# Expert tiles that add into shared rows: waits by token range, and an earlier copy out

## What is computed

```
logits = xf @ Wg.T
topw, topi = top_k(softmax(logits), 2)      # two experts per token
topw = topw / topw.sum(-1)
for e in range(16):
    h = silu(xf @ W1[e]) * (xf @ W3[e])
    out = out + gates[:, e:e+1] * (h @ W2[e])
x = x + out
```

## Time and profile before

| | |
|---|---|
| median of 3 runs | 940.09 us (938.54 to 945.49) |
| the profiled execution | 942.03 us, of which its span 940.3 us |
| mean granted TensorE clock | 0.938 of full |
| busy share PE / DVE / ACT / POOL | 87% / 65% / 42% / 43% |
| adding scatters on POOL (L647) | 80, 124.8 us in all |

### The profile page before, as it was taken

The page is one execution under the profiler, slowest core; times in us unless marked ns, Lnnn a source line. Parts: engine busy times, 40 slices in busy tenths (PEclk is TensorE's granted clock), DMA queues, the critical chain, the costliest instruction groups (busy, mean ns, idle before and its releaser), DMA issues.

```text
span 940.3 us, 19852 instructions
## 1 busy us (share of the span) xinstructions
PE 821.2 (87%) x5656; PEld 737.8 (78%) x5657; DVE 611.1 (65%) x1711; ACT 394.6 (42%) x1070; POOL 406.8 (43%) x583
## 2 busy tenths in 40 slices
PE   6899999999999999999999999986429998888840
PEld 6788999899989998999989999976317877766730
DVE  4446687877878777878787778766465554444520
ACT  5252553634526436245264462532334443333420
POOL 4212134344352533534434435235464456546661
PEclk9799999999999999999999999987559999999985
DMA  8960145172460642725517336086324665656657
GB/s 266 342 217 2 55 170 193 56 247 104 143 236 24 233 158 89 247 71 176 211 36 247 127 120 236 13 257 162 83 66 90 116 105 98 101 91 108 106 59 196
DMA packets 89602, 132.88 MB, mean 141 GB/s; under 512 B 6432, under 2 KB 54240, under 8 KB 89312
## 3 DMA queue, kind: packets, MB, share of 16 engines
q1 hardware_dynamic: 62944, 99.82, 31.9%
q0 software_dynamic: 14848, 19.41, 12.4%
q10 hardware_dynamic: 11776, 13.24, 5.1%
HBM read 37.42 MB, written 99.23 MB: 145 GB/s over the span
## 4 chain that ended last, share of the span: by engine, by line
PE 43%; ACT 15%; DVE 13%; issue 10%; DMA 8%; POOL 6%; ACTq 1%; SPq 1%; POOLq 0%; DVEq 0%
PE ps L656 37%; DMA row_sums<-narrow,sidx 7%; ACT phi L1066 5%; PE ps L663 4%; ACT fT_hi L1079 4%; ACT relu_v L1080 3%; POOL row_sums L647 3%; DVE nmax L1386 1%; DVE xrow_full L1421 1%; DVE smax L1428 1%; DVE row_max_of L1430 1%; DVE prT_lo L1281 1%; ACT pr L1122 1%; ACT qT_hi L1101 1%; DVE stat L1263 1%
## 5 line engine op out<-in xcount | busy, mean ns | idle before, releaser
L647 POOL DMA_INDIRECT row_sums<-narrow,sidx x80 | 124.8, 1560 | 97.9 <-DVE sidx L1611 55.7
L656 PE MATMUL ps<-e_sb,narrow 128*128 x320 | 113.0, 477 | 17.6 <-DVE narrow L1593 15.7
L656 PEld LDWEIGHTS ps<-e_sb,narrow 128*128 128x128 f32 x320 | 55.9, 195 | 38.5 <-issue 21.7
L1066 ACT ACTIVATE phi<-ps,nmax 128x128 f32<-128x128 f32 x256 | 71.3, 379 | 21.0 <-DVE nmax L1386 20.9
L656 PE MATMUL ps<-w_hi,fT_hi 128*128 128x256 f32 x256 | 78.2, 306 | 0.1
L656 PE MATMUL ps<-hT_hi,w_hi 128*128 128x256 f32 x256 | 73.3, 286 | 1.5 <-DVE hT_lo L1281 1.5
L1281 DVE TENSOR_TENSOR fT_lo<-relu_v,fT_hi 128x512 fp32r<-128x512 f32 x64 | 54.9, 858 | 27.4 <-ACT relu_v L1080 27.4
L656 PE MATMUL ps<-hT_hi,w_lo 128*128 128x256 f32 x256 | 72.5, 283 | 0.0
L656 PE MATMUL ps<-hT_lo,w_hi 128*128 128x256 f32 x256 | 72.5, 283 | 0.0
L656 PE MATMUL ps<-w_hi,fT_lo 128*128 128x256 f32 x256 | 72.2, 282 | 0.0
L656 PE MATMUL ps<-w_lo,fT_hi 128*128 128x256 f32 x256 | 72.1, 282 | 0.0
(11 more groups left out here) (269 smaller groups left out, 2699.0 us busy)
## 6 DMA issues: line engine op xcount, KB each, us to landing
expert_rows<-zero_rows SPq DMA_DIRECT2D x16, 4352.0 KB, 15.9
narrow<-expert_rows ACTq DMA_DIRECT2D x80, 136.0 KB
e_sb<-in_E SPq DMA_DIRECT2D x4, 1408.0 KB, 11.5
X<-in_x SPq DMA_DIRECT2D x16, 256.0 KB, 3.0
ctx_raw<-in_ctxT SPq DMA_DIRECT2D x16, 256.0 KB, 16.0
row_sums<-X SPq DMA_DIRECT2D x16, 256.0 KB, 2.2
raw_w<-in_W SPq DMA_DIRECT2D x2, 1024.0 KB, 6.8
e2a_lo<-in_E SPq DMA_DIRECT2D x1, 2048.0 KB
```

What stands on the lines that cost most here:

```text
L647: pool.indirect_dma_start(sum_dram, bass.IndirectOffsetOnAxis(sidx[:, u:u + 1], 0), yg[:, u, :], None, compute_op=ALU.add).then_inc(scatte ...
L656: return pe.matmul(out_, lhsT, rhs, start=start, stop=stop)
L1066: last = act.activation(phi[:, g, h, :], ps[:, g, h * M:(h + 1) * M], ACT.Exp, bias=nmax[:, g, h:h + 1])
```

## The change

1. `added_need` for s-1 and s-2 takes in whether the token ranges meet. For this, DVE computes the numbers of the first and the last row of each slot tile (`edge_i`), POOL gathers these rows from `expert_rows`, PE turns their target rows onto one partition (before tile 1), and DVE compares last row of s with first row of s-k (`meeting_tiles`, after tile 1); a tile that isn't full counts as reaching to the end. SP waits for it (`ranges_ready`) before tile 1.
2. In the last 8 tiles the unconditional wait for s-3 becomes one that holds only if tile s is real.
3. SP issues the first eight row loads in place of ACT.
4. SP waits, for each buffer, only for the real tiles (`landed_need`), and issues all 16 copies. ACT still waits for all scatters and all copies at the end.

```
@@ sync
             sp.wait_ge(x2_stored, 16 * NSEQ)
+            sp.wait_ge(zeroed, 16 * (NSEQ + 1))
             sp.wait_ge(plan_ready, 1)
+            sp.wait_ge(placed, NSEQ * 16 * TOPK * TS)
+            for s in range(GB):
+                tile = sp.value_load(tile_i[0:1, bass.ds(s, 1)], ...)
+                sp.dma_start(xg[:, s, :], row_tiles[...]).then_inc(rows_loaded[s], 16)
...
                 early = s if isinstance(s, int) and s < ADDING else ADDING
-                if early == ADDING:
+                if isinstance(s, int) and s == 1:
+                    sp.wait_ge(ranges_ready, 1)
+                if early == ADDING and not last:
                     v = (u - ADDING) % GB
                     hold(sp, scattered[v], rows_added(s - ADDING, v))
-                near = range(1, min(early, ADDING - 1) + 1)
+                near = range(1, (ADDING if last else min(early, ADDING - 1)) + 1)
...
             for u in range(GB):
-                sp.wait_ge(scattered[u], 16 * (SLOT_TILES // GB + 1))
-            for n in range(0, COPIES, 2):
+                need = sp.value_load(landed_need[0:1, u:u + 1], ...)
+                hold(sp, scattered[u], need)
+            for n in range(COPIES):
                 sp.dma_start(out_parts[n], sum_parts[n]).then_inc(out_stored, 16)
@@ gpsimd
             pool.memset(hid, 0.0).then_inc(hid_zero, 1)
+            pool.wait_ge(edges_ready, 1)
+            pool.wait_ge(placed, NSEQ * 16 * TOPK * TS)
+            for o in range(2):
+                pool.indirect_dma_start(edge[:, o, :], None, row_dram,
+                    bass.IndirectOffsetOnAxis(edge_i[:, o:o + 1], 0)).then_inc(edges_loaded, 16)
@@ tensor, slot_tiles
+                if isinstance(s, int) and s == 1:
+                    pe.wait_ge(edges_loaded, 16 * 2)
+                    for o in range(2):
+                        last_mm = mm(ps[0:1, 1, (2 + o) * P:(3 + o) * P], edge[:, o, D:D + 1], ident[:, :])
+                    last_mm.then_inc(edge_ps, 1)
+                if isinstance(s, int) and s == 3:
+                    pe.wait_ge(edges_read, 1)
@@ scalar
-            act.wait_ge(zeroed, 16 * (NSEQ + 1))
-            act.wait_ge(placed, NSEQ * 16 * TOPK * TS)
...
-            for s in range(GB):
-                load_rows(s, s)
...
-            for n in range(1, COPIES, 2):
-                act.dma_start(out_parts[n], sum_parts[n]).then_inc(out_stored, 16)
             act.wait_ge(out_stored, 16 * COPIES)
@@ vector
+            dve.wait_ge(row_ready, 1)
+            then(dve.tensor_scalar(row_c[:, :], row_g[:, :], float(ROW_TILES - 1), float(P), ALU.min, ALU.mult))
+            dve.tensor_copy(edge_i[:, 0:1], row_c[:, :])
+            dve.tensor_scalar(edge_i[:, 1:2], row_c[:, :], float(P - 1), None, ALU.add).then_inc(edges_ready, 1)
...
+            dve.tensor_scalar(real[:, :], ps[0:1, 1, 0:SLOT_TILES], float(NE), None, ALU.is_lt)
+            dve.tensor_scalar(expert_i[:, :], ..., ALU.min).then_inc(plan_ready, 1)
...
+            dve.scalar_tensor_tensor(added_need[:, ADDING - 1, ADDING:], real[:, ADDING:], 16.0,
+                                     round_of[:, 0:SLOT_TILES - ADDING], ALU.mult, ALU.add)
+            then(dve.tensor_tensor(real_late[:, :], real[:, SLOT_TILES - 2 * GB:SLOT_TILES - GB],
+                                   real[:, SLOT_TILES - GB:], ALU.add))
+            then(dve.tensor_scalar(landed_need[:, :], real_late[:, :], 16.0,
+                                   float(16 * (NT * TOPK // GB + 1)), ALU.mult, ALU.add))
+            def meeting_tiles():
+                dve.wait_ge(edge_ps, 1)
+                dve.tensor_copy(edge_row[:, :, :], ps[0:1, 1, 2 * P:4 * P]...).then_inc(edges_read, 1)
+                dve.wait_ge(edges_read, 1)
+                firsts, lasts = (edge_row[:, o, :] for o in range(2))
+                then(dve.tensor_scalar(no_last[:, :], lasts, 0.0, float(DUMP + NT * P), ALU.is_equal, ALU.mult))
+                then(dve.tensor_tensor(last_row[:, :], lasts, no_last[:, :], ALU.add))
+                for k in range(1, ADDING):
+                    last = dve.tensor_tensor(meeting[:, k - 1, k:], last_row[:, k:], firsts[:, 0:SLOT_TILES - k], ALU.is_ge)
+                then(last)
+                for k in range(1, ADDING):
+                    last = dve.tensor_tensor(meeting[:, k - 1, k:], meeting[:, k - 1, k:], other_expert[:, k - 1, k:], ALU.mult)
+                then(last)
+                for k in range(1, ADDING):
+                    last = dve.scalar_tensor_tensor(added_need[:, k - 1, k:], meeting[:, k - 1, k:], 16.0,
+                                                    round_of[:, 0:SLOT_TILES - k], ALU.mult, ALU.add)
+                last.then_inc(ranges_ready, 1)
```

More of the change, by code:

```diff
@@ L160, in decoder @@
         round_of = sb("round_of", [1, SLOT_TILES])
-        other_expert = sb("other_expert", [1, 2, SLOT_TILES])
+        other_expert = sb("other_expert", [1, ADDING - 1, SLOT_TILES])
+        real = sb("real", [1, SLOT_TILES])
+        real_late = sb("real_late", [1, GB])
+        landed_need = sb("landed_need", [1, GB], I32)
+        row_c = sb("row_c", [P, 1])
+        edge_i = sb("edge_i", [P, 2], I32)
         first_round = sb("first_round", [16, GB, GB])
-        added_need = sb("added_need", [1, 2, SLOT_TILES], I32)
+        added_need = sb("added_need", [1, ADDING, SLOT_TILES], I32)
         early_scope = ExitStack()
@@ L237, in decoder @@
         xg = carve(GB * RW).rearrange("p (u w) -> p u w", u=GB)
+        edge = carve(2 * RW).rearrange("p (o w) -> p o w", o=2)
+        edge_row = carve(2 * SLOT_TILES)[0:1].rearrange("p (o t) -> p o t", o=2)
+        meeting = carve((ADDING - 1) * SLOT_TILES)[0:1].rearrange("p (k t) -> p k t", k=ADDING - 1)
+        no_last, last_row = (carve(SLOT_TILES)[0:1] for _ in range(2))
         yg = carve(GB * D).rearrange("p (u d) -> p u d", u=GB)
@@ L300, in decoder @@
         sidx_ready = sem("sidx_ready")
+        edges_ready, edges_loaded, edge_ps, edges_read, ranges_ready = (sem(n) for n in (
+            "edges_ready", "edges_loaded", "edge_ps", "edges_read", "ranges_ready"))
         rows_loaded = [sem(f"rows_loaded{u}") for u in range(GB)]
@@ L437, in _, with need_of @@
             sp.wait_ge(x2_stored, 16 * NSEQ)
+            sp.wait_ge(zeroed, 16 * (NSEQ + 1))
             sp.wait_ge(plan_ready, 1)
+            sp.wait_ge(placed, NSEQ * 16 * TOPK * TS)
+            for s in range(GB):
+                tile = sp.value_load(tile_i[0:1, bass.ds(s, 1)], min_val=0, max_val=ROW_TILES - 1)
+                sp.dma_start(xg[:, s, :], row_tiles[:, bass.ds(tile, 1), :].rearrange("p t w -> p (t w)"))\
+                    .then_inc(rows_loaded[s], 16)
             def rows_added(s, u):
                 return (s - u) * PER + 16 * 2
+            def need_of(k, s):
+                return sp.value_load(added_need[0:1, k - 1, bass.ds(s, 1)], min_val=16,
+                                     max_val=16 * (SLOT_TILES // GB + 1))
             def slot_tiles(s, u, last):
                 early = s if isinstance(s, int) and s < ADDING else ADDING
-                if early == ADDING:
+                if isinstance(s, int) and s == 1:
+                    sp.wait_ge(ranges_ready, 1)
+                if early == ADDING and not last:
                     v = (u - ADDING) % GB
                     hold(sp, scattered[v], rows_added(s - ADDING, v))
-                near = range(1, min(early, ADDING - 1) + 1)
-                needs = [sp.value_load(added_need[0:1, k - 1, bass.ds(s, 1)], min_val=16,
-                                       max_val=16 * (SLOT_TILES // GB + 1)) for k in near]
+                near = range(1, (ADDING if last else min(early, ADDING - 1)) + 1)
+                needs = [need_of(k, s) for k in near]
                 for k, need in zip(near, needs):
@@ L459, in _ @@
             for u in range(GB):
-                sp.wait_ge(scattered[u], 16 * (SLOT_TILES // GB + 1))
-            for n in range(0, COPIES, 2):
+                need = sp.value_load(landed_need[0:1, u:u + 1], min_val=16 * (NT * TOPK // GB + 1),
+                                     max_val=16 * (SLOT_TILES // GB + 1))
+                hold(sp, scattered[u], need)
+            for n in range(COPIES):
                 sp.dma_start(out_parts[n], sum_parts[n]).then_inc(out_stored, 16)
@@ L641, in _ @@
             pool.memset(hid, 0.0).then_inc(hid_zero, 1)
+            pool.wait_ge(edges_ready, 1)
+            pool.wait_ge(placed, NSEQ * 16 * TOPK * TS)
+            for o in range(2):
+                pool.indirect_dma_start(edge[:, o, :], None, row_dram, bass.IndirectOffsetOnAxis(edge_i[:, o:o + 1], 0))\
+                    .then_inc(edges_loaded, 16)
             def scatter(s, u):
@@ L1195, in _ @@
             act.wait_ge(plan_ready, 1)
-            act.wait_ge(zeroed, 16 * (NSEQ + 1))
-            act.wait_ge(placed, NSEQ * 16 * TOPK * TS)
             def load_rows(s, u):
```

(31 more changed lines are left out.)

## The result

The changed kernel takes 910.66 us (median of 6 runs) against 940.06: ratio 0.969, 95% interval 0.966 to 0.972. That is 29 us less; I had forecast 46 less, with a range of 886 to 906. The profiled execution has a span of 913.6 us.

A forecast was written before the change was run, and what follows sets the result against it. Bound: the chain scatter, landing, SP, next scatter at expert changes. TensorE set free (roughly 33 us) and copies beside dummy tiles (the rest) gave 46 us less: 894 us, range 886 to 906.

The forecast's parts named there:

- The waits that go: Expert stage: 14 of 15 waits on the neighbour tile at expert changes go; only tile 2 still meets its neighbour.
- The wait for s-3: POOL's next limit in the expert stage: 6.45 us per three tiles, just under TensorE's 6.66, so TensorE becomes the bound.
- Rival 1: Expert stage: denser scatters land 0.8 us later, the s-3 wait bounds at 7.2 us per three tiles; end near 906; chance 0.10.
- my bounds for the edge gather: Before tile 1: TensorE's delay from late edge rows, between 0 and +7 us, taken as 0 by the median.
- rival 4: Expert stage: scatter landings stretch to 6.5 us, so the s-3 wait costs more than all that goes; slower than before; chance 0.02.
- The start: Start of the expert stage: moved row loads, transposing products and DVE steps sum to about +1 us for TensorE.
- The copies: End of kernel: the 16 copies begin at 873 us, not 923.56, once tile 70 lands, beside the remaining dummy scatters.
- full addition: Kernel end: DMA work of copies and seven remaining scatters adds up completely, giving an end at 896.6 us.
- free overlap: Kernel end: copies and dummy scatters don't slow each other, giving an end at 891 us.
- My middle value: Kernel end: 893.5 us, taken between 891 and 896.6 and rounded down.
- rival 2: Kernel end: copies run at half speed in one queue and beside scatters; end at 906 us; chance 0.08.
- My last step: Whole kernel: from span 895.2 us to a median of 894, as the profiled execution stood 1.9 us above the median.

The follow-up runs named there:

- ranges_only: Changed kernel with the end of the kernel before: unconditional s-3 waits in the last 8 tiles, waits for all 80 scatters, SP and ACT issuing 8 copies each; 913.92 us, 0.969.
- tail_only: Changed kernel with all tiles of two experts treated as meeting, so only early copy, free dummy tiles and moved row loads remain; 944.71 us, ratio 1.002.
- const_gate: Changed kernel with the last 8 tiles released at once and the copies' needs as constants for this routing, so SP loads nothing there; 903.74 us, ratio 0.959.
- skip_dummy: const_gate without the eight scatters of tiles 72 to 79, final waits lowered to match; 893.18 us, ratio 0.949.
- branch_skip: branch with POOL also branching, so it issues no scatters for tiles 72 to 79 where tile 72 isn't real; 891.82 us, ratio 0.948.
- act_loads: Changed kernel with the first eight row loads given back to ACT; 912.99 us, ratio 0.970.
- branch: Changed kernel with SP loading the copies' eight needs before tile 1, then branching past the last 8 tiles' loads if tile 72 isn't real; 899.83 us, ratio 0.956.
- more_loads: Changed kernel with two more loads and holds of needs per tile in the last 8 tiles, 16 loads in all; 923.98 us, ratio 0.981.
- fit_gates: const_gate with the needs of tiles 8 to 71 also written as constants for this routing, so SP loads nothing in the loop; 899.64 us, ratio 0.956.

## Why the prediction was wrong, step by step

- **The waits that go**: right. Apart from tile 2 (4.74 us) no step of POOL from tile 3 on is over 3.90 us, where 14 had been 4.7 to 6.1. TensorE is busy to 886 us at a granted clock of 1.00, 185.2 from the first row load to its last hidden turn; I had 185.5 (883.3 - 697.8). This alone is the whole gain of the change: ranges_only has it, tail_only has none.
- **The wait for s-3**: the mechanism right, the term of 6.45 us for three tiles under-sized by a little. Had it held, POOL, 5.9 us behind the hidden turn at tile 3, would have closed up to the least of 4.0 by tile 60. It was 7.0 us behind at tile 70. So three tiles cost POOL 6.75 us (150.67 x 3 / 67), just over TensorE's 6.69 (2.231 a tile, I had 2.215). The timeline of POOL, tiles 15 to 19:

```profile
749.81 1.55 POOL L676 DMA_INDIRECT row_sums<-narrow,sidx  x1 [1.65 <-SPq L475]
751.66 1.55 POOL L676 DMA_INDIRECT row_sums<-narrow,sidx  x1 [0.30 <-issue]
753.52 1.55 POOL L676 DMA_INDIRECT row_sums<-narrow,sidx  x1 [0.30 <-DVE sidx L1664]
756.67 1.55 POOL L676 DMA_INDIRECT row_sums<-narrow,sidx  x1 [1.59 <-SPq L475]
758.62 1.55 POOL L676 DMA_INDIRECT row_sums<-narrow,sidx  x1 [0.40 <-issue]
```

  One wait for SP, then two scatters back to back: 6.86 us for three. Rival 1, a landing 0.8 us longer, did not come. The 30 scatters of the changed kernel whose landing is on record took 3.7 to 4.5 us:

  ```profile
  DMA to landing us min/median/max: 3.7/3.9/4.5
  ```

  The kernel before has no scatter's landing on record. Its signs are the 4.06 us of the earlier trace rows and the last scatter, for which ACT waits until 923.5, 3.7 us after its start. I had misread: its landing line, 2.1/3.7/12.4, is of the 16 stores of X and the 16 copies, so neither my bounds for the edge gather nor the 12.4 us in rival 4 say anything of scatters. Tile 70 is at 172.7, against 169.3 to 172.2 in my sum: 0.5 to 3.4 us late.
- **The start**: right in sum, in part by luck. Tile 1's hidden turn is near 12.0 us behind the first row load in most of the runs, 11.0 before (I said +1), but 10.4 in the changed kernel's own profile. I had misread: its 0.63 us at half clock is for two products together, not each. The edge rows landed 6.1 us behind the first row load, before TensorE asked for them at 7.9.
- **The copies**: here the prediction failed, in the step "their waits for real tiles are gone in the last group, so SP has released them by then". A wait that is satisfied still has its load: 24 + 8 loads at about 0.7 us, 22 us of SP, from 874.9 to 897.2. I had counted SP's queue for the row loads and for the issue of the copies, but put the needs at nothing. The copies start 21.9 us late (197.1 against 175.2): 20.5 of it are the loads, since const_gate starts them at 176.6, and 1.4 the later tile 70. At the end the loads cost 10.9 us (213.5 against 202.6 in const_gate), the larger part of the 17.8 by which the end was later than forecast (195.7).
- **Copies beside dummy scatters**: in const_gate, where they do run together, my full addition of DMA work held to 1.4 us (22.2 against 23.6), and the free overlap did not exist. My middle value was 1.7 us short, plus the 3.7 us of POOL's drain, for which I had no term. Even with SP's loads gone the forecast would have been missed by 7 us (end at 202.6 in const_gate, 195.7 in the forecast): 1.4 for the later start of the copies, 1.7 for the addition, 3.7 for the drain.
- **One queue for all 16 copies** (the other half of rival 2): it costs nothing that can be seen. In the changed kernel they take 16.4 us to the end of the span, from two queues 16.7.
- That skip_dummy and branch_skip, at 893 and 892 us, come out near the 894 of the forecast is no merit of it: they leave out work that I had kept. My last step was also rounded up: 895.2 - 1.9 is 893.3, not 894.

Left open: tile 3 to tile 70 takes 150.3 to 151.2 us in the changed kernel, its repeat, ranges_only and act_loads, and 148.3 to 148.8 in const_gate, branch, skip_dummy, more_loads and branch_skip, whose loops have the same instructions. TensorE's pace is the same in both groups; it is POOL that is 7.0 to 7.4 us behind at tile 70 in the first and 4.8 to 5.2 in the second. Each is one profiled execution, and the executions of the changed kernel alone spread over 909 to 917 us. I have no run that explains these 2 us. Loads without the bounds check on SP, which would shorten each, weren't tried.

## What to carry to other kernels

A wait against a loaded value costs its engine the load even when nothing is left to wait for; where a queue must run ahead, count its register loads like any other instruction, load ahead, or branch around them. When work is to be overlapped with work that nobody needs, leave the latter out first: the same DMA engines had to carry both, and eight dummy scatters beside the copies cost 9.7 us, 6.3 beside them and the rest in POOL's drain.

## What the runs showed of the hardware

**POOL's closing drain.** Where the DMA engines are otherwise free it lasts 7.6 us and ends 7.4 us after the last scatter's start, some 3.7 us after ACT has seen that scatter land (before: from 919.5, 7.59 us; after: from 892.4, 7.59 us). There it is hidden under the copies. Where scatters end together with the copies it isn't: const_gate, branch and fit_gates all end 3.7 to 3.8 us after ACT has seen everything land. Why it goes on after the landing no run shows. The row of the closing line for POOL's queue in the changed kernel:

```profile
L94 POOLq DRAIN  x1: 7591/7591/7591, 892.4 to 892.4; - x1
```

**The load of a need into an SP register.** 0.27 us for the load by the median, 0.56 us from one such bounded load to the next, 0.67 to 0.7 on average with the waits between (changed kernel, 874.9 to 897.2 us).

**Adding scatters beside a copy.** With no copies beside it a scatter of 128 rows lands 3.7 to 4.5 us after its start (changed kernel); beside the copies of 4 MB it took 5.5 to 11.3 us (branch), and the copies' packets took 17.4 us in place of 13.8 (const_gate, skip_dummy).
